# Experts' tokens in half tiles of 64, with paired halves of two experts in two column tiles of TensorE

## What is computed

```
logits = xf @ gate_w + gate_b
pb = softmax(logits, axis=-1)
_, idx = top_k(pb, 1)
sel = any(idx[:, :, None] == arange(8)[None, None, :], axis=1)
weights = pb * sel
def expert_step(acc, params):
    w1e, b1e, w2e, b2e, wgt = params          # (256, 1024), (1024), (1024, 256), (256)
    h = gelu(xf @ w1e + b1e)
    y = h @ w2e + b2e
    return (acc + wgt[:, None] * y, None)
out, _ = scan(expert_step, zeros_like(xf), (w1, b1, w2, b2, weights.T))
x = x + out                                    # xf is the layer norm of x
```

## Time and profile before

| | us |
|---|---|
| three runs | 838.01, 838.15, 840.99; median 838.15 |
| profiled execution | 840.62, of which 838.8 span from first to last instruction |
| TensorE busy (matmul) | 770.2 (92%) |
| VectorE busy | 442.7 (53%) |
| ScalarE busy | 255.5 (30%) |
| GpSimd busy | 186.9 (22%) |
| mean granted TensorE clock | 0.967 |
| DMA | 79.68 MB, mean 95 GB/s |

### The profile page before, as it was taken

The page is one execution under the profiler, slowest core; times in us unless marked ns, Lnnn a source line. Parts: engine busy times, 40 slices in busy tenths (PEclk is TensorE's granted clock), DMA queues, the critical chain, the costliest instruction groups (busy, mean ns, idle before and its releaser), DMA issues.

```text
span 838.8 us, 11312 instructions
## 1 busy us (share of the span) xinstructions
PE 770.2 (92%) x4207; PEld 625.8 (75%) x4207; DVE 442.7 (53%) x845; ACT 255.5 (30%) x502; POOL 186.9 (22%) x180
## 2 busy tenths in 40 slices
PE   5998999998989999999999999889886599999996
PEld 4665676687878878887888787645565599999995
DVE  3564678988922953295339532787966311111111
ACT  1533314222211221122122212455642223333331
POOL 3012353533000200020002000455631222222221
PEclk9999999999999999999999999979997699999999
DMA  9962600005000000000000000090122767776640
GB/s 327 385 201 88 264 0 2 1 0 202 2 1 2 2 3 2 2 2 2 2 2 2 2 2 3 8 394 1 51 76 76 255 221 219 227 214 218 205 137 0
DMA packets 20524, 79.68 MB, mean 95 GB/s; under 512 B 3053, under 2 KB 12400, under 8 KB 15664
## 3 DMA queue, kind: packets, MB, share of 16 engines
q1 hardware_dynamic: 17504, 70.44, 24.5%
q0 software_dynamic: 2944, 8.13, 2.5%
HBM read 72.27 MB, written 18.74 MB: 109 GB/s over the span
## 4 chain that ended last, share of the span: by engine, by line
PE 73%; DVE 18%; issue 5%; ACT 3%; DMA 1%; POOL 0%; DVEq 0%; SPq 0%; ACTq 0%; POOLq 0%
PE ps L1133 28%; PE ps L1824 10%; PE ps L1836 9%; PE ps L550 4%; PE ps L501 3%; PE ps L487 2%; DVE f_ha_hi L1233 2%; DVE f_raw L1227 2%; PE ps L1271 2%; DVE head_max L1661 1%; PE ps L579 1%; DVE stats L282 1%; PE ps L1408 1%; DVE c_tok L1662 1%; PE ps L1420 1%
## 5 line engine op out<-in xcount | busy, mean ns | idle before, releaser
L1210 ACT ACTIVATE f_raw<-ps,cols 128x512 f32<-128x512 f32 x96 | 66.2, 690 | 250.2 <-PE ps L1133 218.6
L1133 PE MATMUL ps<-f_hb_hi,fh 128*128 128x512 f32 x256 | 101.2, 395 | 2.5 <-DVE inexact L335 2.5
L1133 PE MATMUL ps<-f_ha_hi,fh 128*128 128x512 f32 x256 | 100.0, 391 | 3.2 <-ACT f_raw L1210 3.2
L1133 PE MATMUL ps<-f_hb_lo,fh 128*128 128x512 f32 x256 | 100.6, 393 | 0.0
L1133 PE MATMUL ps<-f_ha_lo,fh 128*128 128x512 f32 x256 | 99.6, 389 | 0.0
L1824 PEld LDWEIGHTS ps<-xsT,ew 128*128 128x128 f32 x736 | 87.2, 195 | 2.8 <-DVE xsT L1951 1.7
L1824 PE MATMUL ps<-xsT,ew 128*128 128x128 f32 x736 | 87.7, 278 | 1.1 <-DVE xsT L1951 1.1
L1884 ACT ACTIVATE hT<-ps,ew 128x128 f32<-128x128 f32 x184 | 52.5, 369 | 105.6 <-PE ps L1824 105.6
L1836 PE MATMUL ps<-ew,hT 128*128 x368 | 83.1, 379 | 0.0
L1233 DVE CAST f_ha_hi<-f_raw 128x512 fp32r<-128x512 f32 x64 | 32.8, 512 | 89.4 <-ACT f_raw L1210 88.3
L1836 PEld LDWEIGHTS ps<-ew,hT 128*128 128x128 f32 x368 | 68.2, 190 | 8.4
(11 more groups left out here) (241 smaller groups left out, 1290.0 us busy)
## 6 DMA issues: line engine op xcount, KB each, us to landing
ew<-in_ew SPq DMA_DIRECT2D x23, 1028.0 KB, 5.9
fh<-fh_copy SPq DMA_DIRECT2D x2, 4096.0 KB, 15.0
ew<-in_ew SPq DMA_DIRECT2D x1, 8192.0 KB, 23.4
fw<-fw_copy SPq DMA_DIRECT2D x3, 1024.0 KB, 7.1
eb<-in_eb SPq DMA_DIRECT2D x23, 128.0 KB, 3.3
x_res<-in_x SPq DMA_DIRECT2D x4, 512.0 KB, 10.8
rows<-x_res SPq DMA_DIRECT2D x4, 512.0 KB, 3.0
rows<-xn_e SPq DMA_DIRECT2D x4, 512.0 KB, 3.1
```

Of the source, the lines that this page charges most:

```text
L1133: ins = nc.tensor.matmul(out, *((xk, wk) if swap else (wk, xk)), start=(k == 0 and part == 0), stop=(k == w.shape[1] - 1 and part == 1))
L1210: nc.scalar.activation(f_raw[:, m % 3, :], ps[:, ring_bank(n), :], ACT.Silu if m < KH else ACT.Gelu, scale=col(("w1_s", "h1_s", "h2_s")[m ...
```

## The change

- Ranks are split at 64 instead of 128. An expert gets an even number of halves as whole tiles as far as its tokens go, and one more half if the number of its halves is odd. There are 12 tiles that are always whole, 7 that hold two halves of any two experts, and one last half: `MT = NT + E // 2 = 20` slots.
- `ORDER` says which tile each slot computes: slots 0 to 3, the odd ones from 5 to 17, and 18 are whole (`WHOLE`), the even ones from 4 to 16 are pairs (`PAIRED`), slot 19 is the half.
- There are 27 loads of `ew1` (one a whole slot, two a pair) in a ring of six buffers. A pair also loads two b1 rows, each broadcast to 64 partitions (`b1_rows`, one buffer), and two b2 rows.
- In a paired slot `up` swaps its operands: 64 columns of `xsT` are stationary, 512 columns of `ew1` move, and the result lies on partitions 0 to 63 for one half and 64 to 127 for the other. DVE adds b1 (`add_b1`), ACT applies Gelu (two activations of 128x512), PE transposes back with 8 transposes (`turn`), and ACT copies to `hT` (two activations).
- `down` of a pair multiplies 64 columns of `hT` with `ew2` of the first expert and 64 with `ew2_b`, to which DVE has copied the second expert's weights (`second_weights`, 128x2048).
- The order on PE becomes: `up(t+1)`, `turn(t)` if t is a pair, `columns(t+2)`, `down(t)`.
- In the routing each one-hot row has `MH` = 40 entries instead of 23, and DVE has more small steps.

The diff, cut to its core:

```diff
-MT = NT + E - 1
+HS = P // 2
+MT = NT + E // 2
+MH = 2 * MT
+FULL = NT - E // 2
+ORDER = [0, 1, 2, 3]
+for _n in range(FULL, MT - 1):
+    ORDER += [_n, len(ORDER) - (_n - FULL)]
+ORDER += [FULL - 1, MT - 1]
+WHOLE = {t for t, _n in enumerate(ORDER) if _n < FULL}
+HALVES = [2 if FULL <= _n < MT - 1 else 1 for _n in ORDER]
+FIRST_LOAD = [sum(HALVES[:t]) for t in range(MT + 1)]
+SLOT_OF = [t for t in range(MT) for _ in range(HALVES[t])]
+LOADS = len(SLOT_OF)
+LOAD_RING = 6
...
+                    n = FIRST_LOAD[t] + h
+                    r = n % LOAD_RING
+                    e = sp.value_load(expert[0:1, n:n + 1], min_val=0, max_val=E - 1)
+                    experts.append(e)
+                    if n == 1:
+                        sp.wait_ge(e_gathered[0], 16)
+                    if n >= LOAD_RING:
+                        sp.wait_ge(e_h, 2 * (SLOT_OF[n - LOAD_RING] + 1))
+                    sp.dma_start(ew1[r][:], ew1_d[bass.ts(e, 1)].rearrange("a p n -> p (a n)")).then_inc(e_w1[r], 16)
                 if t >= TURN:
                     sp.wait_ge(e_sum, t - TURN + 1)
                 else:
                     sp.wait_ge(rows_stored, 16 * 2 * B)
-                sp.dma_start(eb2[:, u, :], eb2_d[bass.ts(e, 1), :].broadcast_to([P, D])).then_inc(e_b2[u], 16)
+                if t in PAIRED:
+                    if PAIRED.index(t):
+                        sp.wait_ge(e_raw, 2 * PAIRED.index(t))
+                    for h, e in enumerate(experts):
+                        sp.dma_start(b1_rows[half_rows(h), :], eb1_d[bass.ts(e, 1), :].broadcast_to([HS, HID]))\
+                            .then_inc(ld_b1, 16)
+                for h, e in enumerate(experts):
+                    part = half_rows(h) if t not in WHOLE else slice(0, P)
+                    sp.dma_start(eb2[part, u, :], eb2_d[bass.ts(e, 1), :].broadcast_to([part.stop - part.start, D]))\
+                        .then_inc(e_b2[u], 16)
...
+                    if t in PAIRED:
+                        for k in range(KD):
+                            at_ = k * HID + g * 4 * P
+                            for h, n in enumerate(loads):
+                                ins = nc.tensor.matmul(bank[half_rows(h), :], xsT[:, t % 2, k, half_rows(h)],
+                                                       ew1[n % LOAD_RING][:, at_:at_ + 4 * P],
+                                                       start=(k == 0), stop=(k == KD - 1))
...
+            def turn(t):
+                i = PAIRED.index(t)
+                for g in range(2):
+                    pe.wait_ge(e_gelu, 2 * i + g + 1)
                     for q in range(4):
+                        ins = nc.tensor.transpose(ps[:, 2 + 2 * (t % 2) + g, q * P:(q + 1) * P],
+                                                  h_raw[:, (4 * g + q) * P:(4 * g + q + 1) * P], ident)
+                    ins.then_inc(e_turned, 1)
...
                     pe.wait_ge(e_sum, t - 1)
+                if t in PAIRED:
+                    pe.wait_ge(e_w2, PAIRED.index(t) + 1)
                 for k in range(KH):
                     if k % 4 == 0:
                         pe.wait_ge(e_h, 2 * t + k // 4 + 1)
-                    ins = nc.tensor.matmul(ps[:, 6 + t % 2, 0:D], hT[:, t % 2, k, :],
+                    part = slice(0, P) if t in WHOLE else half_rows(0)
+                    ins = nc.tensor.matmul(ps[part, 6 + t % 2, 0:D], hT[:, t % 2, k, part],
                                            ew2[:, bass.ts(e, 1), k, :].rearrange("p a n -> p (a n)"),
                                            start=(k == 0), stop=(k == KH - 1))
+                    if HALVES[t] == 2:
+                        ins = nc.tensor.matmul(ps[half_rows(1), 6 + t % 2, 0:D], hT[:, t % 2, k, half_rows(1)],
+                                               ew2_b[:, PAIRED.index(t) % 2, k, :],
+                                               start=(k == 0), stop=(k == KH - 1))
...
                     up(t + 1)
+                if t in PAIRED:
+                    turn(t)
                 if t + 2 < MT:
                     columns(t + 2)
...
                     act.wait_ge(e_down_full, t - 1)
-                act.wait_ge(e_w1[u], 16 * (t // TURN + 1))
+                if t in PAIRED:
+                    i = PAIRED.index(t)
+                    for g in range(2):
+                        act.wait_ge(e_raw, 2 * i + g + 1)
+                        half = h_raw[:, g * 4 * P:(g + 1) * 4 * P]
+                        nc.scalar.activation(half, half, ACT.Gelu).then_inc(e_gelu, 1)
+                    for g in range(2):
+                        act.wait_ge(e_turned, 2 * i + g + 1)
+                        nc.scalar.activation(hT[:, t % 2, 4 * g:4 * g + 4, :].rearrange("p k n -> p (k n)"),
+                                             ps[:, 2 + 2 * (t % 2) + g, :], ACT.Identity).then_inc(e_h, 1)
...
-            order.step(nc.vector.tensor_tensor(g_first[0][:, E:2 * E], g_first[1][:, E:2 * E],
-                                               g_first[1][:, E - 4:2 * E - 4], ALU.add))
-            ends, starts = g_first[0][:, E:2 * E], g_first[0][:, E - 1:2 * E - 1]
+            order.step(nc.vector.tensor_scalar(g_count[:], total, float(HS - 1), None, ALU.add))
+            order.mark(nc.vector.tensor_scalar(g_first_i[:, 0, E:2 * E], g_count[:], 6, 126,
+                                               ALU.logical_shift_right, ALU.bitwise_and))
+            order.step(nc.vector.tensor_scalar(g_first_i[:, 1, E:2 * E], g_count[:], 6, 1,
+                                               ALU.logical_shift_right, ALU.bitwise_and))
+            dve.wait_ge(bf_ready, 6)
+            order.mark(nc.vector.tensor_copy(g_vals[:, 0, E - 1:2 * E - 1], g_first_i[:, 0, E:2 * E]))
+            order.step(nc.vector.tensor_tensor(g_first[0][:, :, E:2 * E], g_first_i[:, :, E:2 * E],
+                                               g_first_i[:, :, E - 1:2 * E - 1], ALU.add))
+            order.step(nc.vector.tensor_tensor(g_first[1][:, :, E:2 * E], g_first[0][:, :, E:2 * E],
+                                               g_first[0][:, :, E - 2:2 * E - 2], ALU.add))
+            order.step(nc.vector.tensor_tensor(g_vals[:, 2:4, E:2 * E], g_first[1][:, :, E:2 * E],
+                                               g_first[1][:, :, E - 4:2 * E - 4], ALU.add))
+            order.mark(nc.vector.scalar_tensor_tensor(g_vals[:, 1, E - 1:2 * E - 1], g_vals[:, 3, E - 1:2 * E - 1],
+                                                      g_vals[:, 2, 2 * E - 1:2 * E], g_vals[:, 2, E:2 * E],
+                                                      ALU.add, ALU.subtract))
             token_rank(order, LAST)
             dve.wait_ge(g_own, 9 * LAST)
-            order.step(nc.vector.tensor_tensor(g_start[:], g_hot[:], starts.unsqueeze(1).broadcast_to([P, NT, E]),
-                                               ALU.mult))
-            order.step(nc.vector.tensor_reduce(g_startf[:], g_start[:], AX.X, ALU.add))
-            order.step(nc.vector.tensor_tensor(g_tile[:], g_startf[:], g_hi[:], ALU.add))
-            tile_no = con("tile_no", MT).unsqueeze(1).broadcast_to([P, NT, MT])
...
+            order.mark(nc.vector.tensor_tensor(g_tile[:], g_sel[:, :, 2], g_hi[:], ALU.add))
+            order.step(nc.vector.tensor_tensor(g_odd[:], g_hi[:], g_sel[:, :, 0], ALU.is_ge))
+            order.step(nc.vector.tensor_tensor(g_odd[:], g_odd[:], g_sel[:, :, 1], ALU.mult))
+            order.step(nc.vector.tensor_tensor(g_tile[:], g_tile[:], g_odd[:], ALU.add))
+            half_no = con("half_no", MH).unsqueeze(1).broadcast_to([P, NT, MH])
+            nc.vector.tensor_tensor(g_hi_hot[:, :, 0, :], spread(g_tile[:], MH), half_no, ALU.is_equal)\
+                .then_inc(scalar_in, 1)
+            dve.wait_ge(scalar_in, 1)
...
-                .then_inc(place_tile, 1)
+                                    con("count", NT).unsqueeze(2).broadcast_to([P, NT, MH]), ALU.mult)\
+                .then_inc(tensor_in, 1)
             spread_ranks(LAST)
...
-            order.step(nc.vector.tensor_copy(g_places[:].rearrange("p a m -> p (a m)"), ps[:, 6, 0:2 * MT]))
+            order.step(nc.vector.tensor_scalar(g_vals[:, 3, E:2 * E], g_vals[:, 3, E:2 * E],
+                                               g_vals[:, 2, 2 * E - 1:2 * E], None, ALU.add))
+            order.step(nc.vector.tensor_tensor(
+                g_cmp2[:], con("load_no", LOADS).unsqueeze(2).unsqueeze(3).broadcast_to([P, LOADS, 2, E]),
+                g_vals[:, 2:4, E:2 * E].unsqueeze(1).broadcast_to([P, LOADS, 2, E]), ALU.is_ge))
+            order.step(nc.vector.tensor_reduce(g_eid[:], g_cmp2[:].rearrange("p l a e -> p l (a e)"), AX.X, ALU.add))
+            order.step(nc.vector.tensor_copy(g_eid_i[:], g_eid[:]))
...
+            for h in range(2):
+                order.mark(nc.vector.tensor_copy(
+                    g_places[half_rows(h)], ps[half_rows(h), 6, 0:2 * MH].rearrange("p (a h m) -> p a h m", a=2, h=2)
+                    [:, :, h, :]))
```

(24 more changed lines are left out.)

202 lines of the change are left out of this document (111 added, 91 removed).

## The result

| | before | after |
|---|---|---|
| runs | 838.01 to 841.86, median 839.41 us (6) | 831.38 to 834.76, median 834.26 us (6) |
| ratio of the times | | 0.9924, 95% interval 0.9902 to 0.9947 |
| profiled execution, its span | 840.62, 838.8 us | 831.38, 829.6 us |
| TensorE busy | 770.2 us | 756.6 us |
| VectorE, ScalarE busy | 442.7, 255.5 us | 460.2, 247.4 us |

By the ratio over all executions the change makes the kernel faster by 0.76% (0.53 to 0.98%), that is 6.4 us (4.5 to 8.2) of 839.4; the two medians lie 5.2 us apart. A second set on another chip, six runs of the changed kernel and eleven of the one before, gave 0.9914 (0.9883 to 0.9946), 832.81 against 840.74 us. The forecast was 10.0 us less.

The account below looks back on a forecast made before the run. The prediction took TensorE's time per slot to bound the expert stage. Stage -12.9 us and routing +2.9 us gave -10.0, so 838.15 became 828.2 us, with an 8 in 10 range of 823.5 to 837.5 us.

Parts of the forecast that it names:

- the prediction's own signs: In the trace: 20 beats, first transposes waiting for the gather, not the weights' chain, no DMA waits between paired slots.
- Slots: Expert stage: 20 slots instead of 23, 12 whole at 7.25 us, 7 paired at 8.52, one half at 7.25.
- multiplications: Up and down of a paired slot, two tiles fully overlapped: 3.43 + 3.46 = 6.89 us.
- The sentence on L579: Evidence for overlap from 64x64 tiles: 24 records plus one switch in 2.78 and 2.73 us, where serial is 5.18.
- wait for the Identity: In a paired slot, PE waits ahead of down for ACT's copy to `hT`: 0.2 us, bounds 0 and 0.6.
- The stage: All expert slots together: 153.9 us against 166.8, so 12.9 us less.
- Routing: DVE's added work from the ranks to the first gather, paid whole: +2.9 us, bounds 2.2 and 3.8.
- the weights' chain stays hidden with 1.4 to spare: Routing behind the token numbers: this chain grows 1.4 us but had ended 2.8 us ahead of the first gather.
- Cost nothing: DMA and SP's queue in the stage: the added loads cost no time, with between nothing and a quarter to spare.
- the second rival: Weights or b1 come late in the paired slots: 832 to 843 us, chance 0.11.
- The first rival: The two column tiles don't overlap or only in part: up to 48 us more, 876 us; chance 0.07.

Follow-up runs that it names:

- The control: The changed kernel itself run once more on another chip: 832.81 us, ratio 0.9914 to the kernel before.
- v_gather: The changed kernel with each gather issued ahead of the scatter instead of behind it: 832.63 us, ratio 0.9885 to the kernel before.
- v_all: Changed kernel with gathers ahead of scatters, `turn` between the halves of the next up, and the weights' matmuls behind the first two slots' transposes: 829.03 us, ratio 0.9855.
- v_turn_gather: Changed kernel with gathers ahead of scatters and a pair's transposes between the halves of the next slot's up: 826.82 us, ratio 0.9828 to the kernel before.
- v_pool: Changed kernel with gathers ahead of scatters, `turn` between the next up's halves, and one routing product moved from DVE to POOL: 828.34 us, ratio 0.986.
- The longer chain: The changed kernel with ten more small ordered DVE steps ahead of the weights' one-hot rows: ranks to first transposes 18.96 us instead of 16.59.
- more loads: The changed kernel with two more loads of 320 KB of weights in each of slots 4 to 17: 844.15 us against 832.81.
- one tile: The changed kernel with both halves of paired slots writing through one and the same column tile: 881.83 us against 832.81.
- the turned order: The changed kernel with a paired slot's transposes between the two halves of the next slot's up, gathers still behind scatters: ratio 0.9928 to the kernel before.

## Why the prediction was right, and where it was too high

The direction, the range and the mechanism held: 834.26 us lie inside 823.5 to 837.5, 0.9924 lies below 0.995. The size was too large, 10.0 us against 6.4 (4.5 to 8.2), or 7.9 by the traces without the part ahead of the stage. Two of the prediction's own signs came out against it: PE's first transposes wait for the weights' chain and not for the gather, and a wait for DMA, 0.15 us for a gather, stands in the paired part.

*Slots.* 20 slots, and whole ones at 7.25 us: right. A pair with its whole neighbour, 15.77 us by the sum, took 15.81. Its terms: multiplications 6.89, measured 3.49 + 3.55 with the switches inside them and behind; the switch out of the tiles shows as 0.37 us for transposes that take 0.22. (The sentence on L579 gives its 24 records both 2.78 and 2.73 us; only the second is theirs, the first is L501's. The sum of 5.51 us holds.) The other terms: `turn` 0.87; wait for the Identity 0.2, measured 0.22 to 0.23.

*The stage* was to take 12.9 us less and took 10.3. The 2.6 us, in the changed kernel's first profile: 0.8 is the first up, 6.28 us against 5.46. The granted clock from 660 to 670 us is 0.59, where before had 0.76. The control and `v_gather`, `v_all` have a first up of 5.71, 5.72 and 5.85 us, `v_turn_gather` and `v_pool` 6.26 and 6.25, by the two groups of executions told of below, and the profile of before is of the first group. So some 0.3 us seem to come with the change, whose longer routing leaves PE idle longer ahead of it, and 0.5 with the execution. The longer chain bears on it: it is of the first group too, PE stood idle 2.4 us longer, and its first up took 6.23 us. 0.8 is the late gather of slot 5: from down(2) to down(3) 696.57 - 688.36 = 8.21 us, where the two runs with the gathers first have 7.41. The rest, 1.0, is small things: up of slot 18 with 3.77 us, up of the half slot with 3.5 instead of 3.4, the last two downs with 7.12 instead of 6.92, the switches on either side of the first paired up (0.3), and 0.04 us a pair.

*Routing.* +2.9 to the token numbers was forecast. From the ranks to `token` it grew from 6.97 us to 10.08, +3.1. Right in size. The step that failed is the one that followed: "the weights' chain stays hidden with 1.4 to spare". The reserve was misread: the 2.8 us of the earlier trace rows are PE's idle time since its own last matmul, while the weights had ended only 2.0 us ahead of the gather. The chain grew by 1.75 us instead of 1.4 (the three products of one-hot rows and weights take 2.3 us instead of 1.45, PE's matmuls 1.8 instead of 1.1), and the first gather landed in about 5.75 us instead of 6.29. 2.0 - 1.75 - 0.54 is -0.3, as measured. So the total, which was to be +2.9, is +2.83 by two terms that cancel in part: +3.1 up to the gather's start, 0.5 less for the gather, 0.25 more for the weights. The longer chain and the late matmuls show both sides of it.

*DMA.* "Cost nothing" was right for weights and b1: no wait for them shows in the changed kernel's two profiles. (With more loads DVE waits once for b1, 0.9 us; with one tile the second up waits 0.75 us for its weights, 0.2 more than it otherwise waits for DVE.) The bounds were 400 and 290 GB/s of capacity; 327 GB/s at a share of 1.01 is what the experiment showed, so the changed kernel's 281 GB/s leave some 14%, not a quarter. That is a mean of 100 us: as the late gather was under way, from 689 to 694.5 us, DMA moved 388 GB/s at a share of 0.96. The prediction looked at SP's queue alone and not at POOL's, whose gathers share the engines. The row for them (5.3 us to landing) was not read, nor the 7.7 us that they have. This is the mechanism of the second rival with another victim. It cost 0.8 us in the changed kernel's first profile, 6.3 in the turned order and some 11 with more loads.

*The first rival*, no overlap, priced at 876 us: the kernel with one tile measured 881.83, with 7 x 6.88 = 48.2 forecast and 49.0 measured. The Trainium skill, "TensorE: Matmul & The Clock Gate", section Measured speedup vs the span model, has 2.38 for three column tiles of 32; the prediction's estimate from it for two tiles was 1.59. Here it is 7.03 / 3.61 = 1.95 for up. By that estimate the kernel would be at 840.7 us; the measured 834.26 disagrees with it.

*From execution to execution.* The place of the last ranks varies by 5.4 us over twelve profiled executions of nearly the same code up to there, and the granted clock from 600 to 640 us falls into two groups with it: at 0.91 (seven profiles, before and the control among them) the ranks come between 646.06 and 649.44, at 0.95 or 0.96 (the other five, the changed kernel's first among them) between 644.07 and 646.84. That is nearly as large as the whole effect. It is why the ratio stays open by 0.2% either way, and which part of the 1.5 us between 7.9 and 6.4 is chance and which are executions with more late gathers than the profiled one stays open.

## What to carry to other kernels

When tokens, rows or requests are padded to a full tile, halves of two groups can share the array: price them by the records at full overlap plus the way back (transposes, one hand-over, two switches), and check that the queue alternates between the tiles. When a change leaves the bound engine alone for longer transfers, follow every queue that shares the DMA engines, most of all the short ones that are released late and asked for soon; here the gathers lost their cover before the large loads did. A reordering that wins on the bound engine can be worth nothing until the next limit is moved, so try the two together.

## What the runs showed of the hardware

- Two column tiles of 64 columns over all 128 rows, fp32, 512 or 256 moving columns, run at the same time almost without loss: 3.61 against 7.03 us for 16 records. A switch between the full array and the tiles costs about 0.15 us each way: the transposes behind a paired up take 0.37 us instead of 0.22, and a whole down, a paired up and its transposes take 7.41 us, where the pieces without switches (3.46, 3.43 and 0.22) are 7.11.
- Matmuls of different tiles don't keep the queue's order: the first records of both halves start together though two of one stand ahead of the first of the other, and in blocks of sixteen the other tile's first starts beside the thirteenth, ahead of three. In these traces no more than three records were passed over.
- Two waits of TensorE of 1.23 and 0.41 us, close together, were followed by 2 us at a granted clock of 0.50, and the down there took 5.40 us instead of 3.62, so that a gather some 1.2 us late cost over three. With more loads, waits of 3.60 and 0.31 us were followed by a clock of 0.50 too, but waits of 1.53 and 0.42 us by 1.00 throughout and a down of 3.72; so the length of the wait alone doesn't tell.
- With loads of 8 KB rows, b1 and b2 broadcasts, gathers of 2 KB and scatters of 1 KB rows, the 16 DMA engines were full at a mean of 327 GB/s (310 to 356 in shorter stretches), while some 7 us of queued weight loads alone had moved about 400. Gathers then landed in 7.8 us in the median and in 12.4 at most, instead of 5.3.
- DVE copied 128x2048 fp32 from SBUF to SBUF in 1.23 us, half of what I took from L315's combination of integers. The Trainium skill, "VectorE: DVE Perf Modes", section The perf-mode tier table, gives 1227 ns for this copy and 2293 for a combination of two operands; the row agrees to the nanosecond:

```profile
L2075 DVE COPY ew_b<-ew 128x2048 f32 x7 | 8.6, 1227 | 2.6 <-issue 2.6
```
